# Attention pipeline of a cross-attention and mixture-of-experts kernel: its steps in another order on every engine

## What is computed

```python
def _L0_xattn_ref(q, k, v, gamma):          # (4, 512, 512) each, 8 heads of 64 rows
    qk = jnp.einsum('bhdq,bhdl->bhql', qh, kh) * scale
    sm = jax.nn.softmax(qk, axis=-1)
    ret = jnp.einsum('bhql,bhdl->bhdq', sm, vh)
    return gamma * ret.reshape(B, Dv, Lq)
...
x = x + _L0_xattn_ref(_layernorm(x), ctx_2048, ctx_2048, gamma)
x = x + _L0_ffn_ref(_layernorm(x), ...)     # 8 experts, 2 per token, and a shared expert
```

## Time and profile before

| What | us or share |
|---|---|
| Three runs | 898.32, 897.53, 900.61; median 898.32 |
| The profiled execution: its own time, span | 897.0, 895.2 |
| TensorE busy | 850.4 us, 95% |
| VectorE, ScalarE, GpSimd busy | 63%, 56%, 49% |
| DMA | 81.24 MB, mean 91 GB/s |
| Chain that ended last | PE 86%, POOL 5%, DVE 3%, ACT 2%, DMA 2% |

### The profile page before, as it was taken

One profiled execution on the slowest core, in us unless ns is written; L12 is line 12 of the kernel. 1 busy time (PEld: TensorE's weight loads), 2 busy tenths in 40 slices (PEclk: granted clock), 3 DMA queues, 4 the chain that ended last, 5 costly groups with the idle time before them and its releaser, 6 DMA issues.

```text
span 895.2 us, 13754 instructions
## 1 busy us (share of the span) xinstructions
PE 850.4 (95%) x4624; PEld 709.4 (79%) x4624; DVE 568.3 (63%) x819; ACT 504.7 (56%) x862; POOL 438.6 (49%) x422
## 2 busy tenths in 40 slices
PE   4999999999869999999999999999999999999993
PEld 2677777777658888888888888888899999999992
DVE  4999999999625533421312121125899999999991
ACT  4999999889543321121112111114888888888881
POOL 6576777875500000043320000002799999999983
PEclk9999999999979999999999999999999999999996
DMA  9113232241343313000310015444844444344342
GB/s 119 61 72 107 94 140 98 81 152 60 118 141 106 106 48 128 13 2 2 122 23 24 1 69 184 158 168 164 257 78 88 72 81 83 70 84 81 71 71 35
DMA packets 63236, 81.24 MB, mean 91 GB/s; under 512 B 15369, under 2 KB 34825, under 8 KB 63186
## 3 DMA queue, kind: packets, MB, share of 16 engines
q1 hardware_dynamic: 53426, 60.14, 22.0%
q0 software_dynamic: 9760, 20.49, 12.7%
HBM read 53.01 MB, written 27.60 MB: 90 GB/s over the span
## 4 chain that ended last, share of the span: by engine, by line
PE 86%; POOL 5%; DVE 3%; issue 2%; ACT 2%; DMA 2%; POOLq 0%; SPq 0%; DVEq 0%; ACTq 0%
PE scores L1352 9%; PE scores L1353 9%; PE scores L1354 9%; PE bank L1226 5%; PE scores L1217 5%; PE bank L1366 5%; PE bank L1367 5%; PE bank L1368 5%; PE bank L1453 3%; PE bank L1454 3%; PE bank L1452 3%; PE bank L1240 3%; PE scores L1428 3%; PE scores L1430 3%; PE scores L1429 3%; PE bank L1428 3%
## 5 line engine op out<-in xcount | busy, mean ns | idle before, releaser
L1009 DVE TENSOR_TENSOR sg<-scores,sg 128x512 f32<-128x512 f32 x44 | 30.4, 692 | 216.0 <-PE scores L1354 201.8
L1352 PE MATMUL scores<-x_hl,wsp 128*128 128x512 f32 x352 | 137.1, 389 | 0.0
L1354 PE MATMUL scores<-x_hl,wsp 128*128 128x512 f32 x352 | 137.0, 389 | 0.0
L1353 PE MATMUL scores<-x_hl,wsp 128*128 128x512 f32 x352 | 137.0, 389 | 0.0
L608 POOL DMA_INDIRECT slot_rows<-msrc,posi x32 | 33.4, 1045 | 185.4 <-PE scores L1354 178.9
L623 POOL DMA_INDIRECT xg<-x_normed_rows,meta x39 | 40.1, 1029 | 160.5 <-PE scores L1376 141.8
L782 ACT ACTIVATE sg<-scores 128x512 f32<-128x512 f32 x44 | 26.3, 598 | 159.7 <-PE scores L1354 159.7
L677 ACT ACTIVATE pb<-scores,negmax 128x512 f32<-128x512 f32 x128 | 88.1, 695 | 12.2 <-DVE negmax L919 12.2
L789 ACT ACTIVATE hh<-sg 128x512 fp32r<-128x512 f32 x44 | 27.8, 631 | 115.9 <-DVE sg L1009 100.9
L929 DVE TENSOR_TENSOR ptl<-bank,pth 128x512 fp32r<-128x512 f32 x128 | 87.1, 683 | 6.1 <-ACT pth L683 5.6
L919 DVE TENSOR_REDUCE negmax<-scores 128x2 f32<-128x1024 f32 x64 | 77.8, 1215 | 9.3 <-PE scores L1217 8.7
(11 more groups left out here) (175 smaller groups left out, 2224.4 us busy)
## 6 DMA issues: line engine op xcount, KB each, us to landing
wex<-in_L_ffn_w_gate SPq DMA_DIRECT2D x8, 704.0 KB, 4.5
wex<-in_L_ffn_w_up SPq DMA_DIRECT2D x8, 704.0 KB, 5.9
xb<-in_x SPq DMA_DIRECT2D x16, 256.0 KB, 2.8
cn<-in_ctx SPq DMA_DIRECT2D x16, 256.0 KB, 2.7
x_rows<-xb SPq DMA_DIRECT2D x16, 256.0 KB, 2.0
x_normed_rows<-x2n SPq DMA_DIRECT2D x16, 256.0 KB, 2.0
x_normed_transposed<-x2T SPq DMA_DIRECT2D x16, 256.0 KB, 2.0
x_hl<-x_normed_transposed SPq DMA_DIRECT2D x4, 1024.0 KB, 5.2
```

The costliest lines, as they stand in the source:

```text
L1352: te.matmul(bk[:, :], hi, xhi, start=(h == 0), stop=False)
L1353: te.matmul(bk[:, :], hi, xlo, start=False, stop=False)
L1354: ins = te.matmul(bk[:, :], lo, xhi, start=False, stop=(h == HC - 1))
```

## The change

All pieces of work stay the same; their order changes on SP, POOL, ACT, DVE and PE, and with it how many tiles apart the pieces of one step are. `P_BANK` gives pieces other banks, and `inverses`, `rows_T` and `logits` now share bank `bT[2]`. The steps run from i = -2 to NT + 3. Queries are made two tiles ahead of their use and not one. SP loads x two tiles ahead and not four, so that load_x(2) comes behind `small_ones` and load_x(3) in step 1. The first four values pieces of a tile come one step later. `first_tokens` runs in steps 10 to 13. The diff; the old list's `freed` lines are left out (they stand in the print above):

```diff
@@ -217,7 +217,7 @@
         bO, bT = bank[4], bank[5:8]
-        P_BANK = (0, 1, 0, 2, 0, 2, 0, 2)
+        P_BANK = (1, 0, 1, 0, 2, 0, 1, 0)
         bG, bU, bY = bank[0:2], bank[2:4], bank[4:8]
@@ -297,7 +297,7 @@
         def over_tiles(step):
-            for i in range(-4, NT + 3):
+            for i in range(-2, NT + 4):
                 step(i)
         def over_slots(eng, slot, reads_experts=False):
@@ -384,17 +384,15 @@
                 sp.dma_start(meta_d.rearrange("(s p) c -> p s c", p=P), meta[:, :, :]).then_inc(st_meta0, 16)
             def step(i):
+                if there(i - 4):
+                    store_rows(i - 4)
+                    store_columns(i - 4)
+                if there(i + 2):
+                    load_x(i + 2)
+                    load_values(i + 2)
                 if there(i - 3):
                     store_normed(i - 3)
-                if there(i + 2):
-                    load_values(i + 2)
-                if there(i - 3):
-                    store_columns(i - 3)
-                if there(i + 4):
-                    load_x(i + 4)
-                if there(i - 1):
-                    store_rows(i - 1)
-                if i == 7:
+                if i == 8:
                     load_block(0, 0)
                 if i == NT - 4:
                     load_chunk(0)
@@ -405,10 +403,8 @@
             load_values(0)
             load_x(1)
             load_values(1)
-            load_x(2)
             small_ones()
-            load_x(3)
-            for i in range(NT + 3):
+            for i in range(NT + 4):
                 step(i)
             for c in range(2, SC):
                 load_chunk(c)
@@ -571,31 +567,31 @@
                 gp.tensor_tensor(v, v.bitcast(F32), x_hl[:, 0, 0, tt, :, :].bitcast(F32), ALU.subtract).then_inc(g_xl, 1)
             def step(i):
-                if there(i + 1):
-                    queries(i + 1)
-                    keys_hi(i + 1)
-                    queries_hi(i + 1)
+                if there(i - 3):
+                    shift(1, i - 3)
+                if there(i - 2):
+                    scaled(i - 2)
                 if there(i - 3):
                     rows_normed(i - 3)
+                if there(i - 2):
+                    residual(i - 2)
                 if there(i + 1):
-                    queries_lo(i + 1)
                     keys_lo(i + 1)
+                if there(i + 2):
+                    inverse_deviation(0, i + 2)
+                    shift(0, i + 2)
+                    keys_hi(i + 2)
+                    queries(i + 2)
+                if there(i):
+                    spread(i)
+                if there(i + 2):
+                    queries_hi(i + 2)
                 if there(i - 2):
                     inverse_deviation(1, i - 2)
                 if there(i + 2):
-                    inverse_deviation(0, i + 2)
-                if there(i):
-                    spread(i)
-                if there(i + 2):
-                    shift(0, i + 2)
-                if there(i - 1):
-                    scaled(i - 1)
-                if there(i - 2):
-                    shift(1, i - 2)
-                if there(i - 1):
-                    residual(i - 1)
-                if 9 <= i < 9 + TB:
-                    first_tokens(i - 9)
+                    queries_lo(i + 2)
+                if 10 <= i < 10 + TB:
+                    first_tokens(i - 10)
             over_tiles(step)
@@ -686,7 +682,7 @@
                 act.wait_ge(e_R, t + 1)
                 after(act, g_att, t)
-                sc.activation(rgam[:, :], bT[1][:, :], ACT.Copy, scale=gam[:, :]).then_inc(a_Rg, 1)
+                sc.activation(rgam[:, :], bT[2][:, :], ACT.Copy, scale=gam[:, :]).then_inc(a_Rg, 1)
             def low_half(t, s):
@@ -699,7 +695,7 @@
                 act.wait_ge(e_x2T, t + 1)
                 after(act, st_x2T[t % 2], 16 * (t // 2))
                 after(act, e_lg, t - 1)
-                sc.activation(x2T[t % 2][:, :, :], bT[1][:, :].rearrange("p (c t) -> p c t", c=HC), ACT.Copy).then_inc(a_x2T, 1)
+                sc.activation(x2T[t % 2][:, :, :], bT[2][:, :].rearrange("p (c t) -> p c t", c=HC), ACT.Copy).then_inc(a_x2T, 1)
             def logits(t):
                 act.wait_ge(e_lg, t + 1)
@@ -724,42 +720,42 @@
                 if there(i):
                     exps(i, 1, 0)
                     exps(i, 1, 1)
+                    values_hi(i)
                 if there(i - 1):
                     probs_hi(i - 1, 4)
-                    inverses(i - 1)
-                    low_half(i - 1, 0)
-                    probs_hi(i - 1, 5)
                 if i == NT:
                     weights_hi(1)
                 if there(i):
                     exps(i, 2, 0)
                 if there(i - 1):
+                    probs_hi(i - 1, 5)
+                if there(i):
+                    exps(i, 2, 1)
+                if there(i - 1):
+                    low_half(i - 1, 0)
                     probs_hi(i - 1, 6)
-                if there(i):
-                    exps(i, 2, 1)
-                if there(i - 1):
-                    probs_hi(i - 1, 7)
-                if there(i):
-                    exps(i, 3, 0)
                 if there(i - 3):
                     rows_T(i - 3)
                 if there(i):
+                    exps(i, 3, 0)
+                if there(i - 1):
+                    probs_hi(i - 1, 7)
+                if there(i):
                     exps(i, 3, 1)
                     probs_hi(i, 0)
-                if there(i - 1):
-                    low_half(i - 1, 1)
-                if there(i):
                     probs_hi(i, 1)
                 if there(i + 1):
                     exps(i + 1, 0, 0)
+                if there(i - 1):
+                    inverses(i - 1)
+                if there(i + 1):
+                    exps(i + 1, 0, 1)
+                if there(i):
+                    probs_hi(i, 2)
+                if there(i - 1):
+                    low_half(i - 1, 1)
                 if there(i - 3):
                     logits(i - 3)
-                if there(i + 1):
-                    exps(i + 1, 0, 1)
-                if there(i):
-                    probs_hi(i, 2)
-                if there(i + 1):
-                    values_hi(i + 1)
             over_tiles(step)
@@ -950,54 +946,55 @@
                 ve.tensor_tensor(v, v.bitcast(F32), x_hl[:, par, 0, :, :, :].bitcast(F32), ALU.subtract).then_inc(d_xl, 1)
             def step(i):
-                if there(i + 2):
-                    first_norm(i + 2)
+                if there(i - 1):
+                    probs_lo(i - 1, 1)
                 if there(i):
                     maxima(i, 1)
                 if there(i - 1):
                     probs_lo(i - 1, 2)
-                if i == 0:
-                    router_columns()
-                if there(i):
-                    values_lo(i)
+                if there(i - 2):
+                    halves(i - 2, 1)
                 if there(i - 1):
                     probs_lo(i - 1, 3)
                 if i == NT:
                     weights_lo(0)
                 if there(i):
                     maxima(i, 2)
+                if there(i + 2):
+                    first_norm(i + 2)
                 if there(i - 1):
                     probs_lo(i - 1, 4)
-                if there(i - 2):
-                    second_norm(i - 2)
-                if there(i - 1):
-                    halves(i - 1, 0)
+                if i == 0:
+                    router_columns()
+                if there(i):
+                    values_lo(i)
+                if there(i - 1):
                     probs_lo(i - 1, 5)
                 if i == NT:
                     weights_lo(1)
                 if there(i):
                     maxima(i, 3)
                 if there(i - 1):
+                    halves(i - 1, 0)
                     probs_lo(i - 1, 6)
                 if there(i - 2):
-                    aggregate(1, i - 2)
+                    second_norm(i - 2)
                 if there(i + 2):
                     aggregate(0, i + 2)
                 if there(i - 1):
                     probs_lo(i - 1, 7)
-                if there(i - 2):
-                    variance(1, i - 2)
                 if there(i + 2):
                     variance(0, i + 2)
                 if there(i + 1):
                     maxima(i + 1, 0)
+                if there(i - 2):
+                    aggregate(1, i - 2)
                 if there(i):
                     inverse(i)
+                if there(i - 2):
+                    variance(1, i - 2)
+                if there(i):
                     probs_lo(i, 0)
-                if there(i - 1):
-                    halves(i - 1, 1)
-                if there(i):
-                    probs_lo(i, 1)
             over_tiles(step)
@@ -1245,7 +1242,7 @@
                 pe.wait_ge(g_rspr, t + 1)
                 for c in range(QC):
```

(75 more changed lines are left out.)

22 lines of the change are left out of this document (5 added, 17 removed).

## The result

The changed kernel takes **904.98 us** (median of nine runs, 902.47 to 906.78) against 899.08 for the kernel before (nine runs on the same chip, 897.51 to 901.42): a ratio of 1.006, 95% interval 1.0044 to 1.0077. The lower end of the interval lies above the 0.3% that such a measurement can tell, so the kernel is slower, and the time lies in the predicted range. The profiled execution took 902.5 us, with a span of 900.7, so 5.5 more than before in both.

What follows compares the result with a forecast made beforehand. TensorE, busy 95% of the span, was taken as the bound. Terms +3.1 - 0.7 + 0.7 - 1.1 + 1.8 = +3.8 us gave 900.8 for a profiled execution and a median of 902.1 us, range 897.0 to 906.5.

Steps and rivals of the forecast that it cites:

- The start: Up to S3(1): load_x(2) lands late behind the slot table, DVE waits about 3 us; +3.1 us, 3.0 from the load.
- P0(0): First probability transpose of tile 0 on PE, held by ACT's exponentials; laid out at 23.6 us.
- S3(1): Milestone: third scores group of tile 1 on PE; forecast at 30.9 us, against 27.79 before.
- rival 3: PE's new hole at the start lowers the clock, twelve matmuls at half rate: about +2.4, 904.5 us; chance 0.10.
- Two tiles without logits: S3(1) to S3(3): scores are done between PE's waits, 12.98 us a tile instead of 13.33; -0.7 us.
- The even tiles: Twelve tiles, S3(3) to S3(15): changed neighbours on PE cost +0.06 us a tile, no engine stalls; +0.7 us.
- rival 4: ACT's chain to P0 is late by 0.2 to 0.4 us each tile: +2.4 to +4.8, 904.5 to 907; chance 0.08.
- First tokens: Four tiles where POOL also splits x_hl: PE's wait for kl stays in two, 1.8 of 2.9 us; -1.1 us.
- The end: S3(15) to gate_up(0, 0): waits in crowded step 16 make it 20.1 us instead of 18.3; +1.8 us.
- V4: Values pair in step 16 on PE, waiting 2.0 us for a half behind weights_lo(1) on DVE.
- Rival 1: load_x(2) lands by 17.0, so DVE doesn't wait; 3.0 us go, 899.1, no measurable change; chance 0.20.
- Rival 2: No load wait, POOL's stall goes altogether, the end costs no more than before: 895.5 us, faster; chance 0.12.

Runs made afterwards that it cites:

- run 1: Changed kernel with load_x(2) issued ahead of small_ones, as in the kernel before; 901.42 us, ratio 1.002 to the kernel before.
- run 2: Kernel before with load_x(2) moved behind small_ones, ahead of load_x(3); 907.47 us, ratio 1.0083.
- run 6: Changed kernel with the slot table's store moved on SP from small_ones to step 4; 909.35 us, ratio 1.0113 to the kernel before.
- run 5: Changed kernel with load_x(2) ahead of small_ones and weights_lo(1) behind probs_lo 7 on DVE; 897.86 us, ratio 0.999 to the kernel before.
- Old, three: Kernel before with the slot table's store in the shared stage, first_tokens right behind keys_lo and weights_lo(1) behind probs_lo 7; 894.46 us.
- run 8: Kernel before and changed kernel, each with table store in the shared stage, first_tokens behind keys_lo, weights_lo(1) behind probs_lo 7; 894.46 us and 896.70 us.
- run 9: The two kernels of run 8, each with 40 unread identity transposes on PE ahead of its first step; 893.42 us (old order), 894.29 us (new order).
- Run 4: Changed kernel with POOL's first_tokens moved right behind keys_lo(i + 1); 905.41 us, ratio 1.0059 to the kernel before.
- run 3: Changed kernel with 26 unread identity transposes on PE ahead of probs_T(0, 0); 905.51 us, ratio 1.0065 to the kernel before.
- run 7: Kernel before with the slot table's store in SP's step 4, first_tokens behind keys_lo and weights_lo(1) behind probs_lo 7; 901.21 us, ratio 1.0017.

## Why the prediction was right, point by point

**The start: +3.1 forecast, +3.76 measured.** The mechanism of the load held, and runs 1, 2 and 6 show it. The load landed at 19.2 and not at 20.0, so P0(0) came at 22.71 and not at 23.6. But what followed ran at half rate. From P0(0) to S3(1) I had laid out 30.9 - 23.6 = 7.3 us, and 31.55 - 22.71 = 8.84 were needed. I put the 1.5 between them down to the clock, where rival 3 had 2.4; that is argued from my layout, since no profile of the new order went through this stretch at full rate. P0(0) came 0.9 earlier than forecast and the 1.5 behind it were missing from the forecast; that the two errors nearly cancel is luck.

So half of rival 3 came true, which I had given 0.10 as if it took the forecast's place. It came together with the forecast, and it doesn't even need the forecast's hole: in runs 1 and 5, where the holes are 0.67 and 0.64, the clock fell at 20.8 and 20.5. Taking run 1's profile as the start without the load's wait, the load has 31.55 - 28.83 = 2.72 of the 3.76, and 1.04 is left where I had 0.1. The profile of the kernel before is the exception: of all thirteen profiles, in either order, it alone shows no half rate between 16 and 28, by its stretches and by the starts of its matmuls. "Old, three" has the same order there without the table, was at half rate from about 16.5 to 23.4, and reached S3(1) at 29.29, 1.5 later. So part of the +3.76 is a lucky execution before, and not the order. The rule of the Trainium skill that I set beside it (TensorE: Matmul & The Clock Gate, What's actually happening), that the throttled state is the default, agrees with the first scores, after PE's idle start: in the changed kernel their matmuls begin 0.43 apart at 10.83 and 11.26, and 0.24 apart at 15.04 and 15.28. My reason against the rival, that pauses of about 1 us in 15 to 19 had left the clock alone, fell: after pauses of 1.52 and 1.22 the clock was down about 0.9 us into the next one.

**Two tiles without logits: -0.7 forecast, -0.48 measured**, and -0.48 and -0.47 in the pairs of runs 8 and 9. Scores between the waits help, a little less than laid out.

**The even tiles: +0.06 each forecast, +0.10 measured** ((164.59 - 163.40) / 12 in run 8). PE has no idle time in them, and no engine is late, so rival 4 is out. The timeline of PE has the pair that the earlier trace rows couldn't show:

```profile
121.15 0.96 PE L1263 MATMUL bank<-rgT,x2T 128*128 128x9 f32 x8
121.97 0.63 PE L1223 MATMUL bank<-ident,pb 128*128 128x128 f32 x4
122.53 0.50 PE L1214 MATMUL scores<-kh,qh 64*128 64x512 f32 x2
```

Logits before a transpose cost 0.82 and not 0.85, but the transpose behind them costs 0.56 before scores where I had 0.52. The step that failed is small: I priced a neighbour by the pair alone, and what stands one before it counts too. The Trainium skill's rule that a change of tiling mode drains TensorE (TensorEngine Tiling (Array Packing), Key Properties) would have given 0, if it is read as the only price; the measured 1.2 over twelve tiles disagrees with that reading.

**First tokens: -1.1 forecast, -1.1 measured.** The four tiles took 14.51, 13.72, 14.48 and 13.70, so the stall came in exactly two, at their S0:

```profile
171.11 0.50 PE L1214 MATMUL scores<-kh,qh 64*128 64x512 f32 x2 [0.71 <-POOL kl L534]
...
199.32 0.50 PE L1214 MATMUL scores<-kh,qh 64*128 64x512 f32 x2 [0.70 <-POOL kl L534]
```

By run 8, 166.12 - 164.59 = 1.53 stay, of 166.06 - 163.40 = 2.66 before. I had laid out 1.8 of 2.9, both a little too large. Run 4 shows the cause by taking it away.

**The end: +1.8 forecast, +1.9 measured.** V4 waits 2.08 (2.0 laid out), V0(15) 0.73 (1.1) and P0(15) 0.42 (1.1), and ptl adds 0.37. Run 5 shows the wait's place on DVE. By runs 8 and 9 only 0.6 belongs to the order (I had 0.9 for it); the rest is `weights_lo(1)` in the wrong place, and the old order had 0.85 of that too.

**The sum.** The terms measured give +5.2 at gate_up(0, 0) against +3.8 forecast. Of the 1.4 between them the start has 0.7, the even tiles 0.5 and the two tiles without logits 0.2, the other terms nearly nothing. The medians differ by 5.9. They lie above the profiled executions, 2.1 us before (899.08 and 897.0) and 2.5 after (904.98 and 902.5), and the start varies between executions. I had taken the landing as one number with ends of 17.0 and 21.1; but behind the table it differs from execution to execution (14.0 to 18.7 in five profiles), and both medians are medians over it. Rival 1 (the load isn't in the way) is excluded by runs 1 and 2. Rival 2 is excluded too: POOL's stall stayed in two tiles, and even with the load and the wait at the end out of the way (run 5) the new order is no faster than the kernel before by more than the measurement can tell, and in run 8 it stands 2.2 us behind the old order with the same calls moved.

What stays open: which part of the loss belongs to the landing and which to the clock in an average execution. The profile shows one execution of each kernel, run 3 didn't separate the two, and run 9 warms only the very start.

## What to carry to other kernels

Before a step is moved past a DMA of very many small rows, look at what it is queued behind: the price isn't its own issue, but the landing of what stands ahead, and it comes due at the first engine that needs the tile in order. Such a transfer belongs where nothing behind it is wanted soon; run 6 shows that "later" alone isn't enough. And where TensorE starts from idle with waits of 1 us and more between short pieces, put the half rate into the forecast, as a part of the same case and not as a rival of it; a longer hole makes it last longer. Read the kernel before in more than one execution for this: its one profile here had none of it. Two orders can only be compared when each has its odd pieces (the first tokens, the extra weights, the table) in its own best places: here these were worth 6.9 us in the new order and 3.3 in the old, and the order itself cost about 1 to 2.

## What the hardware showed that I had not expected

**The eight-byte rows vary.** The same 4,992 rows took 14.3 us to land in the changed kernel's profile, 15.8 in the old one's, and 15.7, 16.0, 17.6, 18.0 and 19.0 in those of runs 3, 5, 4, 1 and 2. The load behind lands with them, 14.0 to 18.7 us after its issue where 2.8 is the median of all the loads of x, and its issue takes 5.9 to 8.5 us instead of 0.43. In step 4 they took 19.3 and 19.6 (runs 6 and 7), in the shared stage 16.2 to 18.6 (runs 8 and 9), so they are no quicker there.

**Short pauses can be enough for the clock.** At the start it fell in run 1 behind pauses of 1.52, 1.22 and 0.67. In the same run PE went at half rate from 239.5 to about 246, behind a wait of 2.08 us in step 16; in the changed kernel the same wait, ahead of 240.70, left the rate as it was. Runs 3 and 4 had it as well: gate_up(0, 0) came 21.6 to 21.8 us behind S3(15) instead of 20.2. These kernels have the same instructions there, so I take it that one kernel has executions of both kinds; no run shows two of one kernel.

**The recorded clock isn't reliable ahead of its first change.** In run 3 the stretches up to 34 us all read 1.00, while the 26 transposes took 0.18 each (0.09 at full rate, as in the 0.36 of four ahead of a values pair) and the scores pair at 20.86 was followed by the next at 21.29, 0.43 later and not 0.23. At the start of a trace take the clock from the starts of the matmuls.
